# Turning a third of the attention key tiles on VectorE and by SBUF-to-SBUF DMA instead of on TensorE

## What is computed

```python
def _attention(q, k, v):
    logits = jnp.einsum('bqhd,bkhd->bhqk', q, k) / jnp.sqrt(64.)
    mask = jnp.tril(...)
    probs = jax.nn.softmax(jnp.where(mask, logits, neg), axis=-1)
    return jnp.einsum('bhqk,bkhd->bqhd', probs, v)
...
x = x + ga * _L0_attn_ref(h, L0_attn_w_qkv, L0_attn_w_out)
h = _layernorm(x, axis=-1) * (1 + cb) + sb
x = x + gb * _L0_ffn_ref(h, ...)          # y[expert_idx, token], 8 experts, relu, width 512
```

## Time and profile before

| | us |
|---|---|
| median of 3 runs (lowest, highest) | 987.63 (987.43, 989.5) |
| the profiled execution: its time | 984.52 |
| its span, first to last instruction | 982.7 |
| PE busy | 952.1 |
| DVE busy | 708.8 |
| ACT busy | 675.3 |

### The profile page before, as it was taken

One profiled execution on the slowest core, in us unless ns is written; L12 is line 12 of the kernel. 1 busy time (PEld: TensorE's weight loads), 2 busy tenths in 40 slices (PEclk: granted clock), 3 DMA queues, 4 the chain that ended last, 5 costly groups with the idle time before them and its releaser, 6 DMA issues.

```text
span 982.7 us, 19699 instructions
## 1 busy us (share of the span) xinstructions
PE 952.1 (97%) x6851; PEld 747.2 (76%) x6851; DVE 708.8 (72%) x2362; ACT 675.3 (69%) x1245; POOL 110.2 (11%) x125
## 2 busy tenths in 40 slices
PE   3999999999999999999999999999999999999797
PEld 2677777777777777777777777777777777878797
DVE  5788648875788658784887758774887578986554
ACT  2887667666777658675876768666776677764475
POOL 0200001000100010000100010000100010202144
PEclk9999999999999999999999999999999999999899
DMA  3001100120011100110011000210010000005220
GB/s 81 10 14 50 26 21 15 31 51 20 11 36 25 29 18 21 50 26 20 15 32 34 23 23 12 51 26 20 14 31 18 12 8 11 27 14 176 64 64 26
DMA packets 56002, 30.78 MB, mean 31 GB/s; under 512 B 12455, under 2 KB 53203, under 8 KB 55906
## 3 DMA queue, kind: packets, MB, share of 16 engines
q1 hardware_dynamic: 54658, 27.41, 10.5%
q0 software_dynamic: 1248, 2.13, 0.7%
HBM read 18.21 MB, written 11.77 MB: 31 GB/s over the span
## 4 chain that ended last, share of the span: by engine, by line
PE 95%; DVE 2%; ACT 1%; DMA 1%; SPq 0%; issue 0%; POOLq 0%; POOL 0%; DVEq 0%; ACTq 0%
PE ps L803 27%; PE ps L832 25%; PE ps L814 25%; PE ps L782 6%; PE ps L786 3%; PE ps L845 3%; PE ps L956 2%; PE ps L967 2%; PE ps L931 0%; DMA probs<-in_L_wmod_dram 0%; DVE accT L1108 0%; PE ps L885 0%; PE ps L928 0%; DVE stats L1091 0%; PE ps L947 0%
## 5 line engine op out<-in xcount | busy, mean ns | idle before, releaser
L1021 ACT ACTIVATE probs<-probs,neg_max 128x128 f32<-128x128 f32 (+15 forms) x256 | 308.9, 1209 | 98.1 <-DVE neg_max L1179 96.4
L803 PE MATMUL ps<-k_both,q_both 128*128 128x512 f32 (+2 forms) x1280 | 360.2, 397 | 2.0 <-DVE k_both L1155 1.3
L814 PE MATMUL ps<-ident,probs 128*128 128x128 f32 x2176 | 297.7, 273 | 0.2
L1029 ACT COPY pT<-ps 128x512 f32<-128x512 f32 (+1 forms) x428 | 227.2, 564 | 87.6 <-PE ps L814 81.3
L814 PEld LDWEIGHTS ps<-ident,probs 128*128 128x128 f32 x2176 | 255.1, 141 | 42.3 <-issue 10.1
L1172 DVE TENSOR_SCALAR_CACHE_REDUCE probs<-ps 128x512 f32<-128x512 f32 (+1 forms) x384 | 247.0, 665 | 10.8 <-PE ps L803 8.7
L832 PE MATMUL ps<-pT,v_sb 128*64 128x256 f32 (+1 forms) x2304 | 250.0, 370 | 0.0
L803 PEld LDWEIGHTS ps<-k_both,q_both 128*128 128x128 f32 x1280 | 207.8, 190 | 50.5 <-issue 29.0
L832 PEld LDWEIGHTS ps<-pT,v_sb 128*64 128x64 f32 x2304 | 157.4, 137 | 80.5 <-issue 9.2
L707 POOL CAST k_both<-k_both 64x1024 fp32r<-64x1024 f32 x64 | 66.4, 1038 | 751.0 <-DVE k_both L1155 749.0
L1175 DVE CUSTOM_DVE_ANT_0 probs<-ps,causal 128x256 f32<-128x256 f32 (+3 forms) x256 | 130.5, 510 | 2.1 <-PE ps L803 1.2
(11 more groups left out here) (142 smaller groups left out, 569.8 us busy)
## 6 DMA issues: line engine op xcount, KB each, us to landing
x_sorted<-blank SPq DMA_DIRECT2D x19, 458.5 KB, 5.3
rinv_b<-spread_rows SPq DMA_DIRECT2D x128, 64.0 KB, 2.6
spread_rows<-rinv_rows SPq DMA_DIRECT2D x256, 0.5 KB
probs<-in_L_ffn_W_dram SPq DMA_DIRECT2D x1, 2048.0 KB, 11.1
w_pair<-in_L_attn_w_qkv_dram SPq DMA_DIRECT2D x24, 64.0 KB, 2.2
hT<-x_sorted SPq DMA_DIRECT2D x23, 65.5 KB, 1.8
x_sb<-in_L_attn_x_dram SPq DMA_DIRECT2D x4, 256.0 KB, 5.1
wo_pair<-in_L_attn_w_out_dram SPq DMA_DIRECT2D x8, 64.0 KB, 1.8
```

The lines of the kernel that those rows point to most:

```text
L803: m = pe.matmul(ps_ring[:, s.bank, 0:w], q_split[r % 2][:, q0:q0 + P], k_split[r % 2][:, part, k0:k0 + w], start=(part == 0), stop=(part = ...
L814: m = pe.transpose(ps_turn[:, n % TURN_BANKS, P * r:P * r + P], probs[:, g % 2, r, j * P:j * P + P], ident[:])
L1021: act.activation(row, row, ACT.Exp, bias=neg_max[:, g, r:r + 1], accum_out=row_sum[:, g, r:r + 1]).then_inc(exp_done, 1)
L1029: act.copy(pT[:, n % PT_SLOTS, lo:BANK], ps_turn[:, n % TURN_BANKS, lo:BANK]).then_inc(turn_taken[n % TURN_BANKS], 1)
```

## The change

Of the groups 3 to 7 the first 4, 4, 5, 5 and 5 key tiles (the "far" ones, `FAR`) are no longer turned by PE: 23 of a pair's 72 tiles. For each row, once its exponentials are there, DVE transposes those tiles in 32x32 blocks from `probs` into a buffer `staged` (step **shuffle**, L1277 of the kernel after), one instruction for a row of 512 or 640 columns. The blocks are then in the wrong partitions: block (a, b) of a tile must go from the partitions of a to those of b. SP moves them (step **move**, L671): for each half of a group (two rows) 4 x 4 = 16 DMAs, each from 32 partitions to 32 others, 1 or 1.25 KB from each partition, so 32 DMAs for a group, 1280 in all. They land in `turned_far`, which has two buffers, so that a move waits for the pv of the group before the last. `staged` has one buffer: the first shuffle of a half waits until that half of the group before has been moved.

PE takes the near tiles of a group first and the far ones last (`pv_order`), reading them straight from `turned_far`. `pT` shrinks from 16 slots to 5 and `PV_BATCH` from 15 to 8, one of the two `probs` buffers loses 256 columns, and the weights of the two kinds of take change. SP's list gets the moves by planned time, and W1, b2 and W2 stand in that list too. The tables of the last stage live in `staged` instead of `pT`.

```diff
-PT_SLOTS = 16
-PV_BATCH = 15
+PT_SLOTS = 5
+STAGED = 5
+FAR = {3: 4, 4: 4, 5: 5, 6: 5, 7: 5}
+FAR_BUFS = 2
+ISSUE = 380.0
+LAND = 3500.0
+PV_BATCH = 8
-TAKE_ACT = -1500.0
-TAKE_DVE = 0.0
+TAKE_ACT = -400.0
+TAKE_DVE = 900.0
...
+def pv_order(g):
+
+    return list(range(far(g), tiles_of(g))) + list(range(far(g)))
...
-        turns = [(p, g, j) for p, g in groups for j in range(tiles_of(g))]
+        turns = [(p, g, j) for p, g in groups for j in range(far(g), tiles_of(g))]
...
-        probs = sb("probs", [P, 2, 4, S])
+        probs = [sb("probs0", [P, 4, S - QG]), sb("probs1", [P, 4, S])]
+        staged = sb("staged", [P, 2, P // SQUARE, STAGED, 2 * SQUARE])
+        turned_far = sb("turned_far", [P, FAR_BUFS, 2, P // SQUARE, STAGED, 2 * SQUARE])
...
+                if s.kind == "move":
+                    g, u, a = s.key[1:]
+                    m = plan.move_no[p, g]
+                    sp.wait_ge(shuffled, 4 * m + 2 * u + 2)
+                    if m >= FAR_BUFS:
+
+                        q, f = plan.moves[m - FAR_BUFS]
+                        sp.wait_ge(pv_done, plan.order[q, f, far(f) - 1] + 1)
+                    for b in range(P // SQUARE):
+                        sp.dma_start(turned_far[b * SQUARE:(b + 1) * SQUARE, m % FAR_BUFS, u, a, 0:far(g), :],
+                                     staged[a * SQUARE:(a + 1) * SQUARE, u, b, 0:far(g), :]).then_inc(moved[u], 16)
...
+                    if j < far(g):
+                        m_no = plan.move_no[p, g]
+                        if j == 0:
+                            for u in range(2):
+                                pe.wait_ge(moved[u], 256 * m_no + 256)
+                        of_head = turned_far[:, m_no % FAR_BUFS, :, :, j, :].rearrange("p u a (h i) -> p h u a i", h=2)
...
+                elif s.kind == "shuffle":
+
+                    r, m = s.key[2], plan.move_no[p, g]
+                    u, h = r // 2, r % 2
+                    dve.wait_ge(exp_done, 4 * (p * GROUPS + g) + r + 1)
+                    if m and h == 0:
+                        dve.wait_ge(moved[u], 256 * m)
+                    dve.transpose(staged[:, u, :, 0:far(g), h * SQUARE:(h + 1) * SQUARE],
+                                  probs[g % 2][:, r, 0:far(g) * P].rearrange("p (j b i) -> p b j i", j=far(g), i=SQUARE)
+                                  ).then_inc(shuffled, 1)
```

More of the change, by code:

```diff
@@ L98, in __init__ @@
         scores = [(p, g, r, c) for p, g in groups for r in range(4) for c in range(chunks(g))]
-        turns = [(p, g, j) for p, g in groups for j in range(tiles_of(g))]
+        turns = [(p, g, j) for p, g in groups for j in range(far(g), tiles_of(g))]
+        pvs = [(p, g, j) for p, g in groups for j in pv_order(g)]
+        self.moves = [(p, g) for p, g in groups if far(g)]
+        shuffles = [(p, g, r) for p, g in self.moves for r in range(4)]
         parts = [(p, c) for p in range(PAIRS) for c in range(CHUNKS)]
@@ L103, in __init__ @@
         ends = [(PAIRS - 1, i) for i in range(len(parts_of(PAIRS - 1)))]
-        keys = dict(score=scores, turn=turns, pv=turns, out=norms,
+        keys = dict(score=scores, turn=turns, pv=pvs, shuffle=shuffles, out=norms,
                     proj=[(p, c, j) for p, c in parts for j in range(3)], back=ends,
@@ L113, in __init__ @@
         self.number = {key: i for i, key in enumerate(turns)}
+        self.order = {key: i for i, key in enumerate(pvs)}
+        self.move_no = {key: i for i, key in enumerate(self.moves)}
         self.total = {kind: len(of) for kind, of in keys.items()}
@@ L144 @@
                  act=("hi", "value", "take", "exp", "mod2", "wtake"),
-                 dve=("norm", "sum", "lo", "add", "resid", "top", "take", "smalls", "fresh", "pick", "slots", "ends"))
+                 dve=("norm", "sum", "lo", "shuffle", "add", "resid", "top", "take", "smalls", "fresh", "pick", "slots", "ends"))
     FIRST = dict(act=("hi", "value"), dve=("sum", "norm", "lo"))
@@ L183, in ready @@
             if past and k0 < tiles_of(past[1]) * P:
-                behind = at("turn", past[0], past[1], min((k0 + w) // P, tiles_of(past[1])) - 1)
+                behind = at("shuffle", past[0], past[1], key[2]) if far(past[1]) else 0.0
+                over = min((k0 + w) // P, tiles_of(past[1])) - 1
+                if over >= far(past[1]):
+                    behind = max(behind, at("turn", past[0], past[1], over))
             return max(at("score", *key), behind)
@@ L220, in get_from, with move_at, turned_at @@
         return max(self.at("sum", p, g) + PUT, free)
+    def move_at(self, m, u):
+        if (m, u) not in self.moved:
+            p, g = self.moves[m]
+            begin = max(self.at("shuffle", p, g, 2 * u + r) for r in range(2))
+            if m >= FAR_BUFS:
+                q, f = self.moves[m - FAR_BUFS]
+                begin = max(begin, self.at("pv", q, f, far(f) - 1))
+            if u or m:
+                begin = max(begin, self.move_at(m if u else m - 1, 1 - u)[0] + 16 * ISSUE)
+            if begin >= NEVER:
+                return NEVER, NEVER
+            self.moved[m, u] = begin + HOP, begin + HOP + 16 * ISSUE + LAND
+        return self.moved[m, u]
+    def turned_at(self, key):
+        p, g, j = key
+        return self.move_at(self.move_no[p, g], 1)[1] if j < far(g) else self.at("take", *key)
     def part_of(self, p, g):
@@ L241, in transfers @@
         self.blanks = [(i, min(i + BLANK_ROWS, rows // P)) for i in range(0, rows // P, BLANK_ROWS)]
+        for m, (p, g) in enumerate(self.moves):
+            for u in range(2):
+                for a in range(4):
+                    steps.append((self.move_at(m, u)[0] + 4 * ISSUE * a, "move", (p, g, u, a)))
+        p, g = PAIRS - 1, GROUPS - 1
+        steps.append((self.at("score", p, g, 3, chunks(g) - 1), "w1", (p,)))
+        steps.append((max(self.at("turn", p, g - 1, tiles_of(g - 1) - 1),
+                          self.at("shuffle", p, g - 1, 3) if far(g - 1) else 0.0) + HOP, "w2", (p,)))
         quiet = [(p, g) for p in range(PAIRS - 1) for g in range(GROUPS - 4, GROUPS - 1)]
@@ L276, in took @@
                         "rank": 700.0, "total": 400.0}[kind] + switch
+        if kind == "shuffle":
+            return far(key[1]) * P / 0.96 + 100.0
         if kind == "top":
@@ L331, in choose_pe @@
         score_at = place("score", lambda k: (k[2] * chunks(k[1]) + k[3]) / (4.0 * chunks(k[1])))
-        turn_at = place("turn", lambda k: k[2] / float(tiles_of(k[1])))
+        turn_at = place("turn", lambda k: (k[2] - far(k[1])) / float(tiles_of(k[1]) - far(k[1])))
         waiting = 0
         for key in self.ahead["pv"]:
-            if self.at("take", *key) > now:
+            if self.turned_at(key) > now:
                 break
@@ L529, in adaln_block @@
         rows_turned = sem("rows_turned")
+        shuffled = sem("shuffled")
+        moved = [sem(f"moved{u}") for u in range(2)]
         pv_done = sem("pv_done")
```

88 lines of the change are left out of this document (54 added, 34 removed).

## The result

The changed kernel takes **1342.5 us** (median of 4 runs, 1338.0 to 1343.9) against 988.1 for the kernel before: a ratio of 1.358, 95% interval 1.354 to 1.361, or 354 us more. The forecast was 927 us, 908 to 970. It is rival 2, the moves bound the kernel, and by far more than the 1,095 us that it was given.

What follows compares the result with a forecast made beforehand. PE was taken to bound the kernel: from the profiled execution's 984.5 us, -82.1 + 7.8 + 10 + 4 = -60.3 gives 924.2, and the runs' median lay 3.1 us higher: 927 us, range 908 to 970.

Steps and rivals of the forecast that it cites:

- rival 2: Moves on SP's queue bound the kernel and make it slower: at 0.615 us a move about 1,095 us; chance 0.13.
- SP's price of a move: SP's issue time for one move: 0.315 to 0.43 us, at the far end 0.615, taken as 0.36.
- the step that counted 81 us of 99: SP's queue per pair: moves 57.6, puts and gets 19.9, weights 2.0, blanks 1.8, within PE's 99 us.
- Transposes, -82.1: PE's lists lose 736 transposes at 111.5 ns each: -82.1 us, 10.3 in a pair.
- Switches, +7.8: PE switches more often between pv and the rest: 31 more runs at 0.25 us, +7.8 us (0 to 15).
- Far matmuls, nothing: PE's far matmuls read 32-column runs instead of 128-column ones; no cost taken, 8 us if a tenth dearer.
- DVE, 702 and 832 ns: DVE's shuffles of 512 and 640 columns take 702 and 832 ns, at 1.02 ns a column; 86.4 us a pair.
- Rival 1: DVE becomes the bound if its transpose streams at 1.81 ns a column: 945 to 965 us; chance 0.10.
- Waits, +10: Waits for moves before shuffles and the scores behind them: 1.2 us a pair, +10 us (0 to 40).
- rival 3: Waits eat the gain, with pT at 5 slots and a fixed order: 975 us at 6 us more a pair; chance 0.09.
- The end, +4: Half of (7, 7)'s moves queue behind b2's load on SP, landing 12 to 15 us after the last score: +4 (0 to 9).
- Descriptors, 870 to 1,220 us: Within rival 2: by the skill's 0.68 and 0.95 us a transfer, 1280 moves one after another take 870 to 1,220 us.

Runs made afterwards that it cites:

- the bare run: A kernel with none of this one's work, issuing rows of 16 (or 4) DMAs of one form: copies within SBUF took SP 0.62 to 0.63 us of issue.
- bytes: Changed kernel with all 1280 moves, each carrying only the first tile of a group, 256 B a row in place of 1024 or 1280: 1335.8 us.
- free: Changed kernel's order with no moves made and nobody waiting for one; far products read zeros: 935.4 us, ratio 0.947 to the kernel before.
- half: Changed kernel with only the moves of source quadrants 0 and 1 (640 of 1280), other far tiles zero: 953.7 us, ratio 0.966.
- pool: Changed kernel with half 1's moves issued by GpSimd's queue, moves planned at 0.64 (SP) and 0.52 us (GpSimd): 1016.7 us, ratio 1.029.

## Why the prediction was wrong

**The failed step is SP's price of a move: "the nearest in shape ... so 0.315 to 0.43, and at the far end 0.615; I take 0.36".** The runs give 0.63. The 32-row load in the earlier trace rows and the 128x128 load in the earlier trace rows come from DRAM, and no row of the trace before had both ends in SBUF. The choice went by the number of dimensions of the pattern; the bare run shows that to be the wrong likeness, for a plain copy of 32 rows is at 0.63 and a plain load of the same rows at 0.47. At 0.63 SP's issue of a pair, 160 x 0.63 + 23.7 = 125 us, is over PE's 99, and the step that counted 81 us of 99 fell. The prediction's own sign of it was right: an issue time above 0.47, with PE waiting before the far matmuls and DVE before its shuffles. The argument against rival 2, that only three-dimensional and broadcast patterns are dear, fell with it.

**Rival 2 had the mechanism and a third of the size** (110 us slower, measured 354), and its 0.615 for a move, taken from the gets, happens to lie near the true price. 160 x 0.654 + 24.2 for the rest gives 129 us of a pair, near its 122. What it left out is that SP has no move to issue while a pair's groups 0 to 2 run, and waits 20 us: 129 + 20 is 149 of the 153 measured (the mean distance from pair to pair), the rest gaps under 1 us. Over the six whole distances between pairs 1 and 7 that is 6 x 45.0 = 270 us; from pair 7's first projection to the end it takes 336.2 us against 252.7, 84 more, and the start 3, together 357 between the spans (1339.2 - 982.7). Nearly all of these 84 lie before the last score: from there to the end it is 105.5 us, against 102.3. DVE's share of the fault is small: its waits are waits for the queue, since bytes, with the same count of moves, has 278.3 us of them too.

**The lower clock.** Between free and the changed kernel, with the same PE work, PE is busy for 894.6 and 1007.1 us at a mean granted clock of 0.989 and 0.875. So of the 405 us between their spans PE is busy for 112 and idle for 293. The busy time grows nearly as the clock falls (894.6 x 0.989/0.875 = 1011). The prediction did not price this, and how much of the time it costs is not shown: SP's queue alone, with its wait, makes 149 of a pair's 153 us, and PE's slower work falls in part where PE would have waited anyway. Windows of the changed kernel around a stall:

```profile
607.00:610.00 3.00, 3.00 (x28) 2.25 (x25) 0.41 (x3) 2.65 (x4) 0.39 (x1) 1.00 0.87 216
610.00:613.00 3.00, 1.27 (x12) 1.03 (x10) 0.00 (x0) 0.00 (x0) 0.00 (x0) 1.00 0.30 74
613.00:616.00 3.00, 0.97 (x2) 0.50 (x2) 1.96 (x10) 0.80 (x4) 0.00 (x0) 0.69 0.26 68
616.00:619.00 3.00, 2.37 (x13) 1.68 (x14) 2.40 (x10) 3.00 (x11) 0.00 (x0) 0.50 0.22 59
```

PE is idle for most of 610 to 616, and comes back at 0.50, the lower of its two levels (1.2 GHz, not 2.4).

**Transposes, -82.1: too much.** In a pair of free and of before, each record counted up to the start of the next, turns take 18.39 and 28.09 us, 9.7 less, not 10.3. **Switches, +7.8: too little.** Scores, pv and output projection together take 1.9 us a pair more (38.64, 31.19, 2.24 against 37.80, 30.58, 1.83), not 1.0. PE's pair is 100.5 us, not 99.0, and free takes 935 where the sum without waits and end makes 914: 8 x 1.5 = 12 of these 21 us are this, the rest is not taken apart.

**Far matmuls, nothing: right.** Their mean in free is the near ones' (381 and 385 ns, 256 columns):

```profile
L920 PE MATMUL ps<-pT,v_sb 128*64 128x256 f32 x1312 | 161.3, 385 | 0.7 <-ACT pT L1117 0.7
L920 PE MATMUL ps<-turned_far,v_sb 128*64 128x256 f32 x736 | 87.1, 381 | 0.0
```

**DVE, 702 and 832 ns: right.** The shuffles' mean is 776 ns, and (64 x 702 + 96 x 832)/160 is 780. DVE has 84.9 us a pair (86.4 forecast), ACT 73.1 (71.4). Rival 1 is out. The Trainium skill, "Vector Engine (DVE) Microarchitecture Reference", section 3.8, has the transpose front end sustain one element per cycle per lane. The trace agrees as far as it goes: 512 and 640 columns take 668 to 847 ns, which goes with the 1.02 ns a column of this engine's copies and not with 1.81 (1081 and 1312 ns).

**Waits, +10, and rival 3.** With few enough moves to issue (half) they cost 18 us, in the predicted 0 to 40; for the kernel as it was built they are the 407 us over free, which is the failed step again. `pT` at five slots is not what hurts: free has five too, and PE is busy for 100.2 of its pair's 100.5 us. **The end, +4:** from pair 7's first projection to the end, half takes 253.4 us and free 251.1, so some 2 us. In the changed kernel the far products of (7, 7) start 28 us after the last score and not 12 to 15, after 11 us of PE idle, again for moves.

**Descriptors, 870 to 1,220 us: not the limit.** The Trainium skill, "DMA: Bandwidth & Descriptors", section Bandwidth, says that transfers under 64 KB are descriptor-dominated. Its 0.68 and 0.95 us, from which the prediction's 870 to 1,220 us were estimated, are busy time of the DMA engines for loads from DRAM that GpSimd issues. Such time is not what bound this kernel: the DMA engines were at 21.5%, and bytes shows that size did not count. The number of transfers was the trouble, as that rule warns, but in the queue that issues them.

The same page of the Trainium skill, section "Rules for kernel authors", says that spreading DMAs over several queues gives no bandwidth and only saves a sequencer's issue time. pool agrees, since here issue time was what ran short (-326 us).

## What to carry to other kernels

Price a DMA first by its issue: count the instructions of each queue within the stretch that needs them, not over a whole period, and take the time from a row with the same two memories at its ends; where there is none, time 16 of them alone before moving any work there. If a queue is short, fewer and larger transfers (5 for 16 through DRAM, -374 us) did better here than a second queue (-326 us), and bytes were nearly free while the DMA engines were at a fifth (1335.8 against 1342.5 us). An order that is planned for one price is a cost of its own: run it once without the transfers, to know which of the two is measured.
